# Two of eight probability tiles per head: transposed by VectorE in 32x32 blocks and placed by DMA in place of TensorE, in an attention-plus-FFN layer

## What is computed

```python
xn = _layernorm(x, axis=-1)
# attention
qkv = xn @ qkv_w + qkv_b; q, k, v = split, 16 heads of 128
scores = einsum('bhid,bhjd->bhij', q, k) + slope[h] * where(j <= i, -(i - j), -inf)
ctx = einsum('bhij,bhjd->bhid', softmax(scores), v)
attn = ctx @ out_w + out_b
# FFN: w = lut[idx]
h = silu(xn @ lut[gate_idx].T) * (xn @ lut[up_idx].T)
out = x + attn + h @ lut[down_idx].T
```

## Time and profile before

| | us |
|---|---|
| median of 3 runs | 531.51 (531.38 to 532.7) |
| the profiled execution, its own time | 532.76 |
| its span in the trace | 530.9 |
| TensorE matmul busy | 515.0 (97%) |
| VectorE (DVE) busy | 410.5 (77%) |
| ScalarE (ACT) busy | 303.8 (57%) |
| GpSimd (POOL) busy | 340.6 (64%) |
| mean granted TensorE clock | 0.997 of full |

### The profile page before, as it was taken

How to read it: one execution, slowest core, us unless ns; L and a number is a source line. 1 busy time by engine, 2 the same in 40 slices (tenths; PEclk the granted TensorE clock), 3 DMA queues, 4 the chain that set the end, 5 groups by cost and what they waited for, 6 DMA issues and landing times.

```text
span 530.9 us, 10648 instructions
## 1 busy us (share of the span) xinstructions
PE 515.0 (97%) x3216; PEld 465.3 (88%) x3216; DVE 410.5 (77%) x1068; ACT 303.8 (57%) x653; POOL 340.6 (64%) x395
## 2 busy tenths in 40 slices
PE   7898999999999999999999999999999999989998
PEld 7687889998999889988998899988998899878897
DVE  6798787888778887878788877897897869764451
ACT  3566665657564846666565656474666556654330
POOL 3475977578676856686757866795658657872400
PEclk8999999999999999999999999999999999999999
DMA  7300100001000100010001000010000000000001
GB/s 269 111 21 1 40 22 21 2 20 41 0 20 20 40 0 20 0 40 20 20 0 38 21 0 20 20 40 0 20 0 0 20 1 2 1 1 1 1 21 59
DMA packets 7429, 13.14 MB, mean 25 GB/s; under 512 B 1008, under 2 KB 3184, under 8 KB 7280
## 3 DMA queue, kind: packets, MB, share of 16 engines
q1 hardware_dynamic: 7408, 12.88, 7.4%
HBM read 11.83 MB, written 1.05 MB: 24 GB/s over the span
## 4 chain that ended last, share of the span: by engine, by line
POOL 41%; issue 34%; PE 18%; DVE 4%; ACT 1%; POOLq 1%; DMA 1%; DVEq 0%; ACTq 0%
POOL w_ffn L1028 16%; POOL work L1003 15%; POOL pad L1002 3%; POOL qk_w_lo L983 3%; PE ps_s L393 2%; PE ps_s L394 2%; PE ps_s L395 2%; PE ps_u L393 2%; PE ps_u L395 2%; PE ps_u L394 2%; POOL o_w_lo L1017 2%; POOL v_w_lo L988 1%; PE ps_t L512 1%; PE ps_t L395 1%; PE ps_t L394 1%
## 5 line engine op out<-in xcount | busy, mean ns | idle before, releaser
L1028 POOL TENSOR_TENSOR w_ffn<-w_ffn,term 128x1088 f32<-128x1088 f32 x60 | 152.6, 2543 | 0.0
L659 ACT ACTIVATE work<-work,neg_max 128x128 f32<-128x128 f32 (+7 forms) x128 | 98.7, 771 | 35.0 <-DVE neg_max L846 34.9
L666 ACT ACTIVATE p_t_hi<-ps_t 128x512 fp32r<-128x512 f32 (+1 forms) x192 | 86.2, 484 | 37.0 <-PE ps_t L512 35.5
L879 DVE TENSOR_TENSOR p_t_lo<-ps_t,p_t_hi 128x512 fp32r<-128x512 f32 (+1 forms) x192 | 98.9, 542 | 7.9 <-ACT p_t_hi L666 7.8
L1003 POOL TENSOR_SCALAR work<-work,inv_sum 128x128 f32<-128x128 f32 (+7 forms) x128 | 102.2, 799 | 0.0
L846 DVE CUSTOM_DVE_ANT_0 work<-ps_s,alibi 128x128 f32<-128x128 f32 (+7 forms) x128 | 96.1, 751 | 4.1 <-issue 4.1
L1002 POOL TENSOR_TENSOR pad<-entry 128x1 f32<-128x1 f32 x128 | 26.7, 208 | 102.8 <-DVE inv_sum L873 102.3
L512 PE MATMUL ps_t<-ident,work 128*128 128x128 f32 x576 | 84.6, 273 | 7.2 <-DVE p_t_lo L879 6.1
L512 PEld LDWEIGHTS ps_t<-ident,work 128*128 128x128 f32 x576 | 68.5, 140 | 15.5 <-DVE p_t_lo L879 3.9
L393 PE MATMUL ps_u<-p_t_hi,v_hi 128*128 128x512 f32 x192 | 69.5, 362 | 0.0
L393 PE MATMUL ps_s<-qk_hi 128*128 128x256 f32 (+2 forms) x192 | 67.3, 350 | 1.4 <-DVE neg_max L846 1.4
(11 more groups left out here) (125 smaller groups left out, 1171.6 us busy)
## 6 DMA issues: line engine op xcount, KB each, us to landing
qk_raw<-w_qk SPq DMA_DIRECT2D x16, 256.0 KB, 2.6
w_ffn<-idx SPq DMA_DIRECT2D x1, 2176.0 KB, 11.4
v_raw<-w_v SPq DMA_DIRECT2D x8, 256.0 KB, 2.6
o_raw<-w_o SPq DMA_DIRECT2D x8, 256.0 KB, 2.5
out<-acc SPq DMA_DIRECT2D x8, 128.0 KB, 1.7
acc<-x SPq DMA_DIRECT2D x2, 256.0 KB, 2.9
acc<-x SPq DMA_DIRECT2D x1, 512.0 KB, 5.1
term<-b_out SPq DMA_DIRECT2D x1, 128.0 KB, 6.3
```

The source lines that it names most:

```text
L659: act.activation(slot(i), slot(i), ACT.Exp, bias=neg_max[:, col:col + 1], scale=-1.0, accum_out=row_sum[:, col:col + 1]).then_inc(exp_done, 1)
L666: act.activation(p_rows(0, i, g), ps_t[:, room, 0:len(turned(i, g)) * P].rearrange("p (j q) -> p j q", q=P), ACT.Copy).then_inc(p_hi, 1)
L879: dve.tensor_tensor(p_rows(1, i, g), ps_t[:, room, 0:len(turned(i, g)) * P].rearrange("p (j q) -> p j q", q=P), p_rows(0, i, g).bitcast(F3 ...
L1028: pool.tensor_tensor(piece, piece, term[:, :], ALU.add).then_inc(term_added, 1)
```

## The change

**Transposing.** For heads 0 to 14, tiles 6 and 7 (15 of 36 blocks, 4 of 12 groups) are no longer transposed on TensorE. ACT scales them (`norm` on ACT, in step 7: after that step's `exp` it scales tile 6, then come the units' `hi_of`, then it scales tile 7). DVE transposes each tile in 32x32 blocks into a new buffer `blocks` (`turn_blocks`: tile 6 at the end of step 7, just ahead of that step's look-up, tile 7 in step 0 of the next head, right after its `mask`). SP's queue then issues 16 DMAs (32 partitions by 2 KB each, 64 KB, 1 MB a head) that put the blocks on their partitions, into the `lo` half of `p_t` (`move`). In step 5 ACT rounds them to the `hi` half in two instructions of 1024 columns (`upper_hi_of`), after that step's `exp`, and POOL makes `lo` in place in two of 1024 columns (`upper_lo_of`). Head 15 is transposed on TensorE as before.

**Products.** `pv1` of heads 0 to 14 becomes `middle_context` (tiles 4 and 5: 6 products of 256 columns) and `banded_context` (tiles 6 and 7: 8 products of 256 columns, in two halves that each wait for their `upper_lo`), both at step 6 of the next head. Its moving operand is read, and PSUM written, in runs of 64 and 32 columns. Before, `pv1` was 8 products: five of 512 columns, one of 384 and two of 256, in steps 3 and 4.

**Terms.** `term` has two buffers, so that a look-up waits for the addition before the last. Look-ups are in steps 1, 3, 5 and 7, additions in 3, 6, 7 and in step 0 of the next head.

**The rest.** The units' steps are laid out anew; Q has one buffer in place of two (K keeps two); the ALiBi row is halved in place every second head instead of made from `distance` and `slope`, which are gone; POOL clears `blocks` at the start; the weights for Q and K are split in step 6 and the output projection's in step 7; SP's queue issues the 16 moves ahead of the weight loads of the same stretch.

```diff
-TERM_AT = 0
-SUM_AT = 1
+TERM_AT = (1, 3, 5, 7)
+ADD_AT = {3: 0, 6: 1, 7: 2}
+UPPER_AT = 5
+BANDED = 6
+TAKEN = NT - BANDED
...
     STEADY: [
-        (("q1", 0), ("_out0", 0), ("k1", 1), ("_out1", 1), ("nq0", 2), ("_pv1-", 3), ("_pv1", 4),
-         ("v0", 5), ("v1", 6), ("nk0", 6), ("pv0", 7), ("v2", 7)),
-        (("k1", 0), ("q1", 0), ("v3", 1), ("_out2", 1), ("_out3", 2), ("_pv1-", 4), ("_pv1", 4),
-         ("nk0", 6), ("nq0", 6), ("pv0", 7)),
+        (("q1", 0), ("k1", 1), ("nk0", 2), ("_out0", 3), ("nq0", 4), ("_out1", 5), ("_pv1-", 6), ("_pv1", 6),
+         ("v0", 7), ("v1", 7)),
+        (("q1", 0), ("k1", 1), ("nk0", 2), ("_pv0", 2), ("v2", 3), ("nq0", 4), ("_out2", 4), ("v3", 5),
+         ("_out3", 5), ("_pv1-", 6), ("_pv1", 6), ("pv0", 7)),
...
+            def move(n, p):
+                sp.wait_ge(blocks_turned, n * (2 * TAKEN) + p * TAKEN + TAKEN)
...
+                    sp.wait_ge(unit_done, number(n, kind, p, "_pv1"))
+                for a in range(QUADS):
+                    for g in range(QUADS):
+                        sp.dma_start(p_t[1][g * B32:(g + 1) * B32, PT_BANDS + a * BAND:PT_BANDS + (a + 1) * BAND].bitcast(F32),
+                                     blocks[a * B32:(a + 1) * B32, g, :, :, :].rearrange("p j i c -> p (j i c)")
+                                     ).then_inc(blocks_moved, 16)
...
+                    if begin:
+                        pe.wait_ge(p_lo, turn_no(n, p - 1, BANDED - 1, 1))
+                        middle_context(bank, parity_of(p, name))
+                    else:
+                        for chunk in range(CHUNKS):
+                            pe.wait_ge(upper_lo, n * (2 * CHUNKS) + (p - 1) * CHUNKS + chunk + 1)
+                            banded_context(bank, parity_of(p, name), range(4 * chunk, 4 * chunk + 4))
...
+            def norm(n, p, i):
+                act.wait_ge(inv_ready, tile_no(n, p, i) + 1)
+                col = p * NT + i
+                act.activation(slot(i), slot(i), ACT.Copy,
+                               scale=inv_sum[:, col:col + 1]).then_inc(upper_normed, 1)
+            def upper_hi_of(n, p, chunk):
+                act.wait_ge(blocks_moved, n * (32 * MOVES) + (p - 1) * (16 * MOVES) + 16 * MOVES)
+                act.activation(chunk_rows(0, chunk), chunk_rows(1, chunk).bitcast(F32),
+                               ACT.Copy).then_inc(upper_hi, 1)
...
+                        if i == NT - 1:
+                            exp(n, p, i)
+                            norm(n, p, i - 1)
                         for name, step in units_of(kind, p):
                             if step == i and is_split(name):
                                 hi_of(n, p, name, bank_of(kind, p, name), number(n, kind, p, name))
-                        exp(n, p, i)
+                        if i < NT - 1:
+                            exp(n, p, i)
+                        else:
+                            norm(n, p, i)
+                        if i == UPPER_AT and not (kind == FIRST and p == 0):
+                            for chunk in range(CHUNKS):
+                                upper_hi_of(n, p, chunk)
...
+            def turn_blocks(n, p, i):
+                dve.wait_ge(upper_normed, n * (2 * TAKEN) + p * TAKEN + i - BANDED + 1)
...
+                to = blocks[:, :, 0:i + 1, i - BANDED, :].rearrange("p a j c -> p j a c")
+                dve.transpose(to, slot(i).rearrange("p (j a c) -> p j a c", a=QUADS, c=B32)
+                              ).then_inc(blocks_turned, 1)
...
+                        if i == NT - 1:
+                            invert(n, p, i)
+                            if not last_head:
+                                turn_blocks(n, p, BANDED)
+                        if i in TERM_AT:
+                            look_up(n, kind, p, TERM_AT.index(i))
...
+            def upper_lo_of(n, p, chunk):
+                pool.wait_ge(upper_hi, n * (2 * CHUNKS) + (p - 1) * CHUNKS + chunk + 1)
+                rows = chunk_rows(1, chunk)
+                pool.tensor_tensor(rows, rows.bitcast(F32), chunk_rows(0, chunk).bitcast(F32),
+                                   ALU.subtract).then_inc(upper_lo, 1)
```

More of the change, by code:

```diff
@@ new lines, in banded_context @@
+            def banded_context(bank, pr, js):
+                for j in js:
+                    bands = [t[:, PT_BANDS:].rearrange("p (a j i c) -> p a j i c", j=NT, i=TAKEN, c=B32)[:, :, j, :, :]
+                             for t in p_t]
+                    last = three(ps_u[:, bank, TWO:HALF].rearrange("p (i a c) -> p a i c", i=TAKEN, c=B32),
+                                 both(v, slice(None), j, slice(pr * D, pr * D + D)), bands,
+                                 j == 0, j == NT - 1)
+                if j == NT - 1:
@@ L511, in turn @@
                     for b, j in enumerate(turned(i, g)):
-                        last = pe.transpose(ps_t[:, room, b * P:(b + 1) * P],
+                        last = pe.transpose(ps_t[:, room_of(i, g), b * P:(b + 1) * P],
                                             slot(i)[:, j * P:(j + 1) * P], ident[:, :])
@@ L938, in h_lo_of @@
                                   ALU.subtract).then_inc(h_lo_done, 1)
-            invert(PAIRS, 0, -1)
             units = number(PAIRS - 1, LAST, 1, "pv0")
+            zero = PT_BANDS + (NT - 1) * TWO
+            for part in range(2):
+                last = dve.memset(p_t[part][:, zero:zero + P].bitcast(F32), 0.0)
+            last.then_inc(cleared, 1)
             for what, no in TAIL:
                 if what == "turn":
-                    p_lo_of(PAIRS, 0, no, True)
+                    p_lo_of(PAIRS - 1, 1, no)
                 elif what == "gate_up":
```

380 lines of the change are left out of this document (216 added, 164 removed), and 3 rows, old and new, of the table UNITS.

## The result

The changed kernel takes **634.26 us** (median of 4 runs, 632.37 to 637.63) against 532.11 us for the kernel before, run beside it (531.38 to 532.97): a ratio of 1.193, 95% interval 1.190 to 1.196. It is slower by 102 us, and by 64 us more than forecast.

The account below looks back on a forecast made before the run. TensorE, almost never waiting, was taken as the bound. From 532.8 us profiled, +58.8 of new waits and -20.3 of TensorE work gave 571.3, less 1.2 for the median of runs: 570 us, range 518 to 588.

Parts of the forecast that it names:

- A: The forecast itself: new TensorE waits of 5.5 to 11 us a pair, 550 to 588 us; chance 0.53.
- TensorE's work: Transposes dropped, less dearer products: 2.7 us less a pair of heads over 7.5 pairs, -20.3 us.
- (a): Head start, p = 0: DVE's queue frees q1's bank at about 7.3 us, so nk0 waits 2.5 us.
- (b): Bands, p = 0: DVE reaches mask 5's end at 16.4 us; TensorE waits 1.1 and 1.0 us.
- (c): p = 1 heads: TensorE waits 0.9 for v0's bank, 1.6 for q1's bank, 1.3 at the bands.
- DVE's new operations: Two transposes a head, of 896 and 1024 columns, priced like a mask at 1.0 and 1.14 us.
- D: Rival: a new operation dearer than its nearest row; transposes 605 us, moves above 620, banded matmuls 610; chance 0.08.
- The moves: SP's 16 moves a head, 0.34 to 0.47 us each, last landing at most 2.6 us later: hidden.
- The step that failed: Engine pricing: POOL, 71% busy in the pair, has room for subtractions; a DVE look-up takes 0.77 us alone.
- The second term buffer removes a wait that has 1.6 us in all: Look-ups on DVE: listed among edits costing nothing on the path, removing a wait of 1.6 us in all.
- B: Rival, faster: TensorE's new waits stay under 2.7 us a pair, 511 us with none to 530; chance 0.22.
- C: Rival, half: TensorE's new waits of 3.1 to 5.5 us a pair, 533 to 550 us; chance 0.12.

Follow-up runs that it names:

- run 1: Changed kernel with both DVE transposes cut to their first 128 columns: 615.49 us.
- run 2: Changed kernel with POOL's additions of FFN terms cut from 1088 to 64 columns: 579.92 us.
- run 5: Changed kernel, whole, with POOL's additions placed ahead of the weight splits in their step: 599.48 us.
- run 17: Changed kernel with DVE's look-ups and ALiBi halvings both in the form that also writes an accumulator: 19 us faster than 634.26 us.
- run 7: Kernel before with only the second term buffer and the new steps of look-ups and additions: 565.80 us, ratio 1.061.
- run 4: Changed kernel with ACT's roundings and POOL's subtractions of the top tiles cut to 16 of 256 columns a band: 602.92 us.
- the reordered one: Changed kernel with additions ahead of weight splits, banded products behind step 7's scores, and both DVE transposes in step 7: 592.05 us, ratio 1.111.

## Why the prediction was wrong

The direction was right, and so were the places of the two waits that were forecast. The time was not: 570 against 634, outside the range (588) and outside A's own. By its steps, against the sum table:

- **TensorE's work**, -20.3 forecast, -16.7 measured; -12.8 if the short spacings, of which fewer are left, are counted as they ran. Banded matmuls start 0.12 us apart (306.60, 306.72), as taken.
- **(a), (b), (c), the waits**, +58.8 forecast. At the places named: `nk0` 31.4, bands 26.3, `q1` 4.1, together 61.8. `nk0` waits 2.24 us a head (2.5 and 1.6 forecast), the bands 1.75 (2.1 and 1.3). (a) comes out of the trace: `q1`'s bank is free 7.4 us after the head's start (280.45 to 287.81), 7.3 forecast (its terms add up to 7.5). It left out ACT's chain beside it, which run 1 showed. In (b) the size is right in part by luck: mask 5 ends 21.4 us after the start (at 301.85), where 16.4 was forecast, behind a held look-up and a held ALiBi halving, and TensorE came to the bands some 4 us late too. With the additions short (run 2) the three places have 53.3 us: some 8 of the 61.8 are the additions' doing.
- **DVE's new operations**, transposes 1.14 and 1.0 us after the overlap, measured 1.17 and 1.02 (1238 and 1094 ns less 0.07). Right. D's case for them (2.0 and 2.3) did not come. The estimate made with the 311 ns of the Trainium skill, "VectorE: DVE Perf Modes", section "The three transpose paths", was 4.7 us a head, and 2.2 was measured, for float32: an instruction of 128 columns takes 0.30 us in run 1, but eight such tiles in one instruction 1.24.
- **The moves.** 16 a head took 10.02 us on SP's queue, 0.63 each where I had 0.34 to 0.47, and landed 2.0 us after issue. ACT's rounding has 0.0 us of idle before it (the row of L762 above): hidden, as forecast.
- **The step that failed: POOL "is 71% busy in the pair and has room", and the look-up at "0.77 alone".** The row behind it said 1.03 on the mean, and I noted that some are held up and then priced them as free. POOL's additions neither grew nor gained in number (2540 ns, 2543 before); they were put next to each other and ahead of a scaling, and DVE's `tensor_scalar` cannot pass them. Their short version gives back 54 us, their order alone 35 (run 5), of the 64 that were missing. Taking the hold away by the form gives 19, after paying 0.55 us more for each look-up (run 17). The new places cost without it too: 34 us in the kernel before, with look-ups no longer than they were (run 7). In the changed kernel the two overlap, and no run splits its 64 us between them.
- **"The second term buffer removes a wait that has 1.6 us in all".** This took a move of the order for a mere buffer, and the one buffer also kept look-ups and additions apart. The move has no term in the forecast. Alone it costs 34 us (run 7). In the changed kernel it is worth 16 of the 102 (618 with the terms in their old places). The two parts alone, 34 and 86, are 120; together 102.
- **The clock** was in no term. Slow work rose by 23.9 us. A forecast of 60 us of new waits on a TensorE that had none should have had a term for it, though not one in proportion to the waits: run 2 keeps 69.6 us of waits and only 7 of the 23.9, and run 4 has 25.5 us fewer waits and keeps 20.

The sum then reads: 532.8 - 16.7 + 61.8 + 26.7 (waits not foreseen: 88.5 less 61.8) + 23.9 + 3.9 = 632.4 us for the profiled execution.

B, the case for faster, needed under 2.7 us of new waits a pair; the waits of A came. C did not come, and of D's three cases none did, though a move took 0.63 us and not 0.47 at most. **What stays open:** no version tried is as fast as the kernel before. The fastest with the whole computation is the reordered one, 592 us; with the additions spread and both holds taken away by the form, and so without the table's factor, 569. There TensorE still waits 59.5 us, 16.3 for POOL's scaling, and I tried no version that takes the subtractions of the top tiles off POOL.

## What to carry to other kernels

Busy share says what an engine has to do, not when it is free: for each instruction that is moved, look at the one that it now stands ahead of. Where a group's mean is well above its fastest member (1.03 us against 0.84 here), find what holds the slow ones before pricing any of them, since a change that moves the two together pays the long price each time. And a kernel whose TensorE never waits can lose twice by its first waits: once by the wait, and again by the clock behind it.

## What the hardware showed that I had not expected

- A `tensor_scalar` on DVE that starts in a POOL addition ends some 0.6 us behind it: 2.92 us for 0.84. Work is held by overlap, not by neighbourhood: spreading the additions out made more look-ups long (28 over 2.5 us, from 17). With an accumulator output it takes 1.40 us (1088 columns, uint8 in) and 1.22 (1024, float32 in) beside POOL's work as well as alone, with a read-out of 0.08; POOL's addition takes 2.53 on the mean beside it. DVE's 32x32 transposes are not held either.
- More TensorE work made the kernel faster: 64 us of repeated products, mostly in the waits, 9 us less in all, mean clock 0.984 for 0.949 (one run).
- Transposes of 1024 float32 columns in 32x32 blocks on DVE take 1.24 us each (15 of them), 0.15 us a 128-column block, and one of 128 columns by itself 0.30 (run 1), against 0.10 on TensorE.
